# Weighted sums of a two-direction graph attention: the order of the steps on three engines, and transposes in bf16

## The reference, cut to what matters

```python
def seg_softmax(att, idx, n):
    m = jax.ops.segment_max(att, idx, num_segments=n)
    e = jnp.exp(att - m[idx])
    s = jax.ops.segment_sum(e, idx, num_segments=n)
    return e / (s[idx] + 1e-16)
...
att = seg_softmax(att, col, n)
att_i = seg_softmax(att_i, row, n)
res = (v * att[:, :, None]).reshape(-1, H * DK)
res = jnp.concatenate([res, e0], axis=1)
res_i = (v_i * att_i[:, :, None]).reshape(-1, H * DK)
res_i = jnp.concatenate([res_i, e0], axis=1)
agg = jax.ops.segment_sum(res, col, num_segments=n) + jax.ops.segment_sum(res_i, row, num_segments=n)
```

## Time and profile before

| | us |
|---|---|
| median of 3 runs | 4485.64 |
| lowest and highest | 4477.07 and 4495.2 |
| the profiled execution, time | 4489.73 |
| the profiled execution, span of its instructions | 4488.0 |
| one group of the sums, first to first | about 3.7 |
| sums, two passes of 104 groups | about 771 |

### The profile page before, as it was taken

How to read it: one execution, slowest core, us unless ns; L and a number is a source line. 1 busy time by engine, 2 the same in 40 slices (tenths; PEclk the granted TensorE clock), 3 DMA queues, 4 the chain that set the end, 5 groups by cost and what they waited for, 6 DMA issues and landing times.

```text
span 4488.0 us, 57931 instructions
## 1 busy us (share of the span) xinstructions
PE 2749.5 (61%) x13804; PEld 1878.1 (42%) x13804; DVE 2543.2 (57%) x5123; ACT 1624.9 (36%) x4283; POOL 2727.8 (61%) x2589
## 2 busy tenths in 40 slices
PE   3200005555555782067777869886777878876598
PEld 1000004333453451023444447774444457765346
DVE  7645545555440003434999975557999955552753
ACT  1111100000021110013666657775666657763031
POOL 3777777777677776846777734446777724446100
PEclk6555557777787896588999989998999989997598
DMA  8333349333433544387999955557899945554000
GB/s 338 145 141 141 137 133 256 105 105 105 102 125 108 208 155 145 67 225 230 276 276 275 275 140 143 141 143 212 273 271 272 257 111 142 140 131 128 13 1 29
DMA packets 763466, 742.24 MB, mean 165 GB/s; under 512 B 385207, under 2 KB 650639, under 8 KB 763232
## 3 DMA queue, kind: packets, MB, share of 16 engines
q1 hardware_dynamic: 640820, 395.52, 30.7%
q0 software_dynamic: 115760, 316.99, 23.9%
q10 hardware_dynamic: 6672, 27.26, 1.5%
HBM read 481.29 MB, written 267.14 MB: 167 GB/s over the span
## 4 chain that ended last, share of the span: by engine, by line
DVE 23%; PE 21%; issue 19%; POOL 10%; DVEq 7%; DMA 4%; SPq 2%; ACT 1%; POOLq 0%; ACTq 0%
DVE BIGR L1244 11%; POOL AR L1467 6%; PE ps L575 5%; DVE AR L1264 5%; DVEq L1260 4%; PE ps L870 3%; PE ps L879 3%; POOL rec_src L462 2%; DVE BIGR L555 1%; DMA AR<-typ_x 1%; PE ps L2047 1%; PE ps L1846 1%; PE ps L1853 1%; DVE AR L546 1%; DMA BIGR<-in_L_ffn_w 1%
## 5 line engine op out<-in xcount | busy, mean ns | idle before, releaser
L1220 POOL DMA_INDIRECT AR<-kv_tab,META x832 | 792.4, 952 | 270.2 <-issue 252.1
L1467 POOL TENSOR_TENSOR AR<-AR 128x896 f32<-128x896 f32 x208 | 351.2, 1688 | 522.1 <-ACT AR L1527 522.1
L437 POOL DMA_INDIRECT rec_dst<-AR,slot_e x400 | 441.4, 1103 | 185.6 <-issue 121.7
L1444 DVE TENSOR_TENSOR BIGR<-BIGR,ps 128x260 f32 x832 | 353.5, 425 | 303.9 <-PE ps L1500 155.2
L1244 DVE TENSOR_REDUCE BIGR<-ps 128x8 f32<-128x1024 f32 x416 | 507.5, 1221 | 16.4 <-PE ps L1353 1.1
L462 POOL DMA_INDIRECT rec_src<-AR,slot_e x400 | 422.3, 1056 | 125.3 <-issue 121.7
L575 PE MATMUL ps<-AR 128*128 128x256 f32 x832 | 303.9, 530 | 289.2 <-issue 198.6
L529 POOL DMA_INDIRECT AR<-xn_tab,META x416 | 397.2, 955 | 132.6 <-issue 121.6
L1500 PE MATMUL ps<-AR 128*128 128x260 f32 x1664 | 426.2, 400 | 80.0 <-POOL AR L1467 70.3
L575 PEld LDWEIGHTS ps<-AR 128*128 128x128 f32 x832 | 210.7, 265 | 383.0 <-issue 323.4
L1500 PEld LDWEIGHTS ps<-AR 128*128 128x128 f32 x1664 | 298.7, 191 | 170.4 <-DVE BIGR L1444 127.1
(11 more groups left out here) (409 smaller groups left out, 5818.1 us busy)
## 6 DMA issues: line engine op xcount, KB each, us to landing
v_dst<-AR SPq DMA_DIRECT2D x104, 384.0 KB, 4.1
AR<-v_dst SPq DMA_DIRECT2D x104, 384.0 KB, 3.5
v_src<-AR SPq DMA_DIRECT2D x104, 384.0 KB, 4.9
AR<-v_src SPq DMA_DIRECT2D x104, 384.0 KB, 3.5
AR<-in_W_qvk SPq DMA_DIRECT2D x44, 608.0 KB
rec_dst<-BIGR ACTq DMA_DIRECT2D x1, 26624.0 KB, 90.3
rec_raw<-AR SPq DMA_DIRECT2D x40, 640.0 KB, 3.0
AR<-rec_raw POOLq DMA_DIRECT2D x40, 640.0 KB, 4.3
```

The costliest lines, as they stand in the source:

```text
L437: pool.indirect_dma_start(rec_tab[0], bass.IndirectOffsetOnAxis(ap=slot_e[0][:, c * CC + k:c * CC + k + 1].bitcast(U32), axis=0), RD[s][0] ...
L1220: pool.indirect_dma_start(KVR[s][:, u, 0:KV], None, kv_tab, bass.IndirectOffsetOnAxis(ap=META[o][:, g * U + u, 0:1].bitcast(U32), axis=0)) ...
L1444: ve.tensor_tensor(a, a, PS[4 + u][:, 0:SROW], ALU.add).then_inc(sem("add"), 1)
L1467: pool.tensor_tensor(v, v, VB[s][:, :, D:SROW].unsqueeze(3).to_broadcast([P, U, H1, DK]), ALU.mult).then_inc(sem("pv"), 1)
```

## The change

The three lists of the sums are put in another order. On PE the lookup of group k+2 stands ahead of the sums of group k. On DVE the argument of k+2 stands ahead of the additions of k. On ACT the exponentials are taken for group k+1 in step k, where they were taken for k. Besides, the transposes of the one-hot matrices read the upper halves of the f32 words as bf16 (zeros and ones lose nothing) and write bf16 to PSUM, and the copy from PSUM reads bf16. Counts of instructions per group stay as they are.

```diff
+        OT2 = [PS[s][:, 0:U * P // 2].bitcast(BF16) for s in range(2)]
...
-                ins = pe.transpose(PS[s % 2][:, u * P:(u + 1) * P], OH[s][:, u, :], ident[:, :])
+                ins = pe.transpose(OT2[s % 2][:, u * P:(u + 1) * P], halves(OH[s][:, u, :]), identb[:, :])
...
-            pipe(ve, [(0, add), (2, argument)])
+            pipe(ve, [(2, argument), (0, add)])
...
-            pipe(pe, [(0, sums), (2, lookup), (3, turn)])
+            pipe(pe, [(2, lookup), (0, sums), (3, turn)])
...
-                act.activation(OT[s % 2].rearrange("p u n -> p (u n)"), PS[s % 2][:, :], ACT.Copy).then_inc(sem("ot2"), 1)
+                act.activation(OT[s % 2].rearrange("p u n -> p (u n)"), OT2[s % 2], ACT.Copy).then_inc(sem("ot2"), 1)
...
-            pipe(act, [(1, copies), (0, exponentials), (3, onehot)])
+            pipe(act, [(1, copies), (1, exponentials), (3, onehot)])
```

## The result

| | before | after |
|---|---|---|
| median, us | 4483.45 (4 runs, 4477.07 to 4495.2) | 5455.0 (4 runs, 5451.78 to 5462.32) |
| ratio to before | | 1.217, 95% interval 1.214 to 1.220 |
| span of the profiled execution, us | 4488.0 | 5450.8 |
| first to last matmul of the sums, two passes, us | 766 | 1731 |
| us a group, pass 0 and pass 1 | 3.69 and 3.72 | 8.39 and 8.39 |

The change made the kernel 971 us slower. The time is in the sums: their two passes take 965 us more (1731 - 766), and all the rest is as it was.

A forecast was written before the change was run, and what follows sets the result against it. TensorE and VectorE, both nearly full, were taken to hold the sums at 3.71 us a group. A ring of 7.38 us adds 3.67 a group, other edits 0: 4485.64 + 763 = 5249 us, range 5105 to 5440.

The forecast's parts named there:

- a ring at half clock: Rival for the sums: TensorE's clock at half nearly throughout, 8.41 us a group, +978 us, 5463 us; chance 8%.
- The ring through the sums: Sums of k-1, one-hot of k+3, copy and lookup of k+2, sums of k run end to end, once per group.
- legs: Ring's four start-to-start times at full clock: copy to lookup 0.63, lookup 1.0, sums to one-hot 2.05, one-hot to copy 2.16.
- The clock: TensorE's dense work in the ring goes 60% at half speed, lengthening 5.84 us a group to 7.38.
- The wait itself: TensorE idles 2.2 us a group after its transposes, before the next lookup, until ScalarE's copy releases it.
- the range's ends: Low end: 40% at half speed with short legs, 5106 us; high end: 90% with long legs, 5441 us.
- The mean grant: Expected profile sign: granted clock 0.65 to 0.8 in the sums, with L1502 averaging 500 to 650 ns.
- my upper mark: The 650 ns upper end expected for the mean of L1502, a record of the sums, which was 400 before.
- Transposes in bf16: At most 131 us could go on TensorE, but they lie in its idle 2.2 us beside the one-hot: 0.
- The exponential ahead: On ScalarE it waits behind its own copy, but the next one-hot waits longer for the sums anyway: 0.
- the argument ahead: On VectorE additions queue behind an argument waiting for the lookup, but their sums follow that lookup too: 0.
- The rival on the faster side: Ring doesn't close, weighed-value wait goes, VectorE's 3.55 us a group sets the pace: -33 us, 4452 us; chance 3%.

The follow-up runs named there:

- e1: Kernel before with only TensorE's lookup of k+2 moved ahead of the sums of k: 878 us slower than before, ratio 1.167.
- e9: Changed kernel with eight one-hot buffers instead of four in pass 0 only: 747 us slower than before, 6.21 us a group in pass 0, 8.34 in pass 1.
- e6: Changed kernel with eight extra, unused bf16 matmuls a group on TensorE ahead of the transposes: 662 us slower than before, ratio 1.149.
- e8: Changed kernel with sixteen extra, unused bf16 matmuls a group on TensorE ahead of the transposes: 591 us slower than before, ratio 1.112.
- e10: Changed kernel with a fifth, unused activation of 0.39 us in each one-hot on ScalarE: 986 us slower than before, ratio 1.220.
- e4: Kernel before with only the transposes and their copy in bf16, all orders as before: -1 us against before, ratio 1.000.
- e11: Changed kernel with transposes and their copy back in f32, the three reorderings kept: 872 us slower than before, ratio 1.193.
- e3: Kernel before with only the exponentials taken one group ahead on ScalarE: 240 us slower than before, ratio 1.045.
- e5: Kernel before with only the argument moved ahead of the additions on VectorE: 488 us slower than before, ratio 1.092.
- v1: Changed kernel with shorter leads: lookup and argument one group ahead, exponentials before copies, transposes before sums: -1 us against before, 3.71 us a group.
- v4: Short-lead version of the changed kernel, sixteen window numbers per VectorE load, f32 transposes: 45 us slower than before, ratio 1.011.

## Why the prediction was wrong, point by point

The direction and the mechanism held, and the size was too small: 5249 us forecast, 5455 measured, just above the upper end of 5440 and beside the rival of a ring at half clock, 5463, to which I gave 8%.

**The ring through the sums: right.** e1 alone brings it about, and e9 opens it without moving a step in any engine's order. Its length by legs was right at both speeds: 5.84 forecast and 5.97 read in e6 and e8 at full, 8.41 forecast and 8.4 to 8.6 read in the kernel after at half. Copy to lookup takes 0.73 us in the loop where the unrolled part had 0.63, 0.1 x 208 = 21 us; at full speed the sums' leg is 0.12 longer than forecast, too, and the lookup's 0.09 shorter.

**The clock: wrong in its size, and this is the step that failed.** "Here the stretch between bursts is longer, so I take 60%": it was 98% of the bursts. 0.38 x 2.57 x 208 = 203 us, which is the whole error (5455 - 5249 = 206). The share came from the first graph layer, and the layer differs in a way that I overlooked. There a burst comes every 5.05 us whatever its length, so the wait depends on the burst before: 1.36 us ahead of the burst at 885.99, which takes 1.97 us, and 3.12 us behind it, ahead of the one of 3.44 us at 891.07. Between 790 and 1200 us each of the 28 bursts of 1.97 us is followed by a longer one, and 27 of the 46 that take over 3 us by one of 1.97. In the ring the wait is the same after a slow burst, 2.64 us before the lookup (median of the kernel after), since the one-hot and the copy start only when the burst is over. That this is what took the share from 60% to 98% is argued from these rows; no run isolates it. The clock did rise in the ring, but late, when a burst was nearly or quite over, and fell again before the next sums, so the full speed went to the wait. That the ring keeps step with the clock isn't the reason, since e10 broke the step and the bursts stayed slow. The wait itself was mis-sized too, at 2.2 us. And I gave the range's ends as 40% and 90%, which left out the 98% that my own rival, the ring at half clock, stood for: I had priced it right, and then weighed it at 8%.

**The mean grant says little about work.** I forecast 0.65 to 0.8 in the sums and 500 to 650 ns for L1502. Measured were 0.60, just under my mark, and 645 ns, just inside it, and yet the sums ran at half speed throughout: 645 ns is what a record of the sums takes there, so my upper mark couldn't tell a mixed clock from a half one, and all the full clock lay in the waits.

**Transposes in bf16, 0 us: right as far as it went, wrong in the changed kernel.** I named TensorE's idle time as their cover and put at nothing what their shorter work does to the clock. e4 has 0, e11 99 us.

**The exponential ahead and the argument ahead, 0 us each: right in this kernel.** e11 has both and e1 neither, and their sums take the same, 1632 and 1633 us. In another order neither is free: 240 us alone (e3) and 488 (e5). "So nothing is held up" was true only because the lookup stood first.

**The rival on the faster side** rested on VectorE's 3.55 us. v1 has no wait of VectorE left and takes 3.71 us: the floor was the mean of its four steps, not the shortest one.

**Of the 971 us**: 208 x (5.97 - 3.70) = 472 us are the ring, what a full clock would have left by the turns of e8, and about 500 the clock (208 x 2.4, from 5.97 to 8.39). The least that a run measured is 591 (e8).

## What to carry to other kernels

Before moving a step ahead in one engine's order, write down for each buffer who frees it and who fills it, and follow the chain through every engine's own order: a wait on a group as old as the buffers are many becomes a ring of one group as soon as each engine's order lets the next step in only behind it. Then ask what the new idle time does to TensorE's clock: a ring that leaves it waiting should be priced at both levels, and the low one not weighed lightly; here it was the low one. Work that TensorE does for nothing in a wait can pay (e6 to e8), and a saving in a wait can cost (e11).

## What the runs showed of the hardware that I had not expected

- In a ring of 8.4 us the full clock came only while TensorE was waiting. The mean grant was 0.60, and 102 of 104 bursts of sums took half speed. With another length of the ring (e10) the clock rose more often, but again only 2.9 us or more after a burst had begun.
- The mean granted clock answers by degrees to added work: 0, 4, 8 and 16 extra matmuls of 256 columns a group gave 0.60, 0.71, 0.85 and 0.89, and took the loss from 971 to 591 us.
- 0.39 us more on a path of 8.4 us cost 0.02 us a group, while full-speed stretches moved onto the lookup (e10).
- Transposes bear on the clock: f32 in place of bf16 raised the grant from 0.60 to 0.67 and made the changed kernel 99 us faster (e11).
- One load of sixteen numbers into VectorE's registers holds up the next addition by 1.27 us (v4), one of four by 0.5 (v1).
